# Output pieces inside the recurrent steps, Toeplitz blocks loaded in the mixing stage, first spectrum evacuated by VectorE

## What is computed

```
# layer 0: Fourier mixing and a multilayer perceptron
xf = rfft2(layernorm(x));  o1 = relu(xf @ w1 (per frequency, 8 blocks of 12) + b1)
xs = irfft2(o1);           x = xs + x + gelu(layernorm(xs) @ mlp_w1 + mlp_b1) @ mlp_w2 + mlp_b2
# layer 1: gated Toeplitz convolution along rows and along columns
u, v = silu(srms(x) @ Wu + bu), silu(srms(x) @ Wv + bv)
x = (u * (toeplitz_h(v) + toeplitz_w(v))) @ Wo + bo + x    # coefficients from a small network of positions
# layers 2 and 3: two bidirectional GRUs over the 256 places, forwards and backwards
inner, z = split(layernorm(x) @ w_in.T)
y = silu(bigru_f(inner) + flip(bigru_b(flip(inner)))) * silu(z)
x = x + y @ w_out.T
```

## Time and profile before

| | us |
|---|---|
| median of three runs (1133.48 to 1138.72) | 1134.02 |
| the profiled execution, its own time | 1135.26 |
| its span, first to last instruction | 1133.1 |
| mixing, perceptron, Toeplitz, input of the second layer from last | up to 222 |
| steps of the two recurrent layers | 222 to 645 and 687 to 1109.5 |
| busy: PE 1026.5, DVE 857.8, ACT 783.1, POOL 78.6 | |

### The profile page before, as it was taken

How to read it: one execution, slowest core, us unless ns; L and a number is a source line. 1 busy time by engine, 2 the same in 40 slices (tenths; PEclk the granted TensorE clock), 3 DMA queues, 4 the chain that set the end, 5 groups by cost and what they waited for, 6 DMA issues and landing times. The chain is left out here.

```text
span 1133.1 us, 55089 instructions
## 1 busy us (share of the span) xinstructions
PE 1026.5 (91%) x22248; PEld 850.9 (75%) x22248; DVE 857.8 (76%) x5635; ACT 783.1 (69%) x4511; POOL 78.6 (7%) x149
## 2 busy tenths in 40 slices
PE   3685897899999999999999899999999999999997
PEld 2462687588888888888888667888888888888876
DVE  3645346688888888888888766888888888888883
ACT  4323472687778877777777737878877777777772
POOL 1003130000000000001100000000000001100000
PEclk9577897755555555555555566555555555555555
DMA  4002320000000000000000000000000000000001
GB/s 129 2 2 28 80 62 1 6 4 4 4 3 4 3 4 4 4 4 4 4 3 4 3 6 3 4 4 4 4 3 4 3 4 4 3 4 4 4 4 29
DMA packets 14940, 13.01 MB, mean 11 GB/s; under 512 B 12370, under 2 KB 13843, under 8 KB 14396
## 3 DMA queue, kind: packets, MB, share of 16 engines
q1 hardware_dynamic: 14684, 9.49, 3.7%
HBM read 8.65 MB, written 0.83 MB: 8 GB/s over the span
## 5 line engine op out<-in xcount | busy, mean ns | idle before, releaser
L1103 DVE TENSOR_TENSOR_SCAN L3s_h_hi<-L3s_renew,L3s_terms 96x32 f16<-96x32 f32 x512 | 114.5, 224 | 64.5
L1103 DVE TENSOR_TENSOR_SCAN L2s_h_hi<-L2s_renew,L2s_terms 96x32 f16<-96x32 f32 x512 | 114.4, 224 | 64.6
L1211 PE MATMUL L2s_reset_sum<-L2s_h_hi,L_w_hidden 97*128 97x8 f16 x2048 | 139.8, 179 | 11.7 <-DVEq L1080 0.4
L1211 PE MATMUL L3s_reset_sum<-L3s_h_hi,L_w_hidden 97*128 97x8 f16 x2048 | 139.7, 179 | 11.7 <-DVEq L1080 0.4
L1211 PEld LDWEIGHTS L2s_reset_sum<-L2s_h_hi,L_w_hidden 97*128 97x128 f16 x2048 | 94.6, 107 | 62.3 <-DVE L2s_h_hi L1103 13.7
L1211 PEld LDWEIGHTS L3s_reset_sum<-L3s_h_hi,L_w_hidden 97*128 97x128 f16 x2048 | 94.5, 107 | 62.3 <-DVE L3s_h_hi L1103 13.9
L1159 ACT ACTIVATE L3s_terms<-L3s_cand 96x16 f32<-96x16 f32 x512 | 111.6, 218 | 37.9 <-DVE L3s_cand L1089 6.0
L1159 ACT ACTIVATE L2s_terms<-L2s_cand 96x16 f32<-96x16 f32 x512 | 111.6, 218 | 37.7 <-DVE L2s_cand L1089 5.9
L1211 PE MATMUL L3s_cand_sum<-L3s_h_hi,L_w_hidden 97*128 97x8 f16 x2048 | 131.3, 175 | 4.5 <-DVE L3s_h_hi L1103 3.2
L1211 PE MATMUL L2s_cand_sum<-L2s_h_hi,L_w_hidden 97*128 97x8 f16 x2048 | 131.3, 175 | 4.3 <-DVE L2s_h_hi L1103 2.9
L1211 PE MATMUL L3s_keep_sum<-L3s_h_hi,L_w_hidden 97*128 97x8 f16 x2048 | 130.0, 174 | 0.0
(11 more groups left out here) (262 smaller groups left out, 3233.5 us busy)
## 6 DMA issues: line engine op xcount, KB each, us to landing
L_wih_raw<-in_L_wih SPq DMA_DIRECT2D x2, 1152.0 KB, 11.9
lagged<-in_L_w SPq DMA_DIRECT2D x1, 1296.0 KB
L_w_hidden_raw<-in_L_whh SPq DMA_DIRECT2D x2, 576.0 KB
stream<-in_x SPq DMA_DIRECT2D x2, 384.0 KB, 4.0
out<-stream SPq DMA_DIRECT2D x4, 192.0 KB, 2.1
l_idft<-in_idft SPq DMA_DIRECT2D x1, 400.0 KB
rpe_lw<-in_rpe_lw SPq DMA_DIRECT2D x1, 384.0 KB
lagged<-coefs SPq DMA_DIRECT2D x16, 24.0 KB, 2.0
```

The lines of the kernel that those rows point to most:

```text
L1103: e.tensor_tensor_scan(flat(h_hi[g][0:C, x]), flat(renew[g][:, x]), flat(terms[g][:, x]), 0.0, ALU.mult, ALU.add).then_inc(hi_ready[g], 1)
L1211: return e.matmul(dst, weights.hidden[0:rows, wp, GATES * (2 * g + j) + gate, :], rhs, start=False, stop=False, skip_group_check=True)
```

## The change

- The Toeplitz blocks are stored and loaded in the mixing block: SP waits for `rpe.finished`, stores, waits for ScalarE's clearing of `lagged` (an activation with scale 0, behind its spreads, in place of GpSimd's memset), and issues the 16 transfers. GpSimd's bias addition stays in `mlp`, now first on its list.
- ScalarE waits for the raw weights alone (`raw_loaded`); VectorE evacuates the 8 banks into `spectrum`.
- Toeplitz: results are copied into `values` without transposing (the turning back reads them with a stride of 16 floats instead), and the turning back of a = 0 goes ahead of the products of a = 1; ScalarE's saving goes with it.
- Recurrent steps: GpSimd has nothing left. For chunks from step 128 on, VectorE does 12 pieces of 96x64 in the next chunk, one between `kept_part` and `new_state` of 12 of the 16 half-steps: 4 additions of directions, 4 products y times gate, 4 products with the sigmoid; ScalarE does 4 sigmoids, each behind a tanh. Only the last chunk's pieces stand behind the last step. The output block keeps the projection and the residual sum; the spare products go. `s_tok` lies in `lagged`.

```diff
 # mix_frequencies, SP, VectorE and ScalarE
-                e.dma_start(w_raw, d["L0_w1"]).then_inc(w_loaded, 16)
+                e.dma_start(w_raw, d["L0_w1"]).then_inc(raw_loaded, 16)
...
                 e.dma_start(idft[:], d["idft"]).then_inc(w_loaded, 16)
+                e.wait_ge(rpe.finished, 1)
+                e.dma_start(coefs.rearrange("(m c) a l -> c m a l", m=CHUNKS), coef[:]).then_inc(lagged_loaded, 16)
+                e.wait_ge(lagged_loaded, 16)
+                e.wait_ge(spread_ready_s, CLEARED)
+                for octet in range(8):
+                    mine = slice(octet * SIDE, (octet + 1) * SIDE)
+                    for axis in range(2):
+                        e.dma_start(lagged[mine, axis, :, mine], lagged_layout(coefs, octet, axis)).then_inc(lagged_loaded, 16)
...
+                for b in range(BATCH):
+                    e.wait_ge(transformed, b + 1)
+                    e.tensor_scalar(spectrum[:, :, b], banks[b][0:C, 0:2 * FREQS], affine[:, 0:1], None, ALU.mult).then_inc(evacuated, 1)
...
-                e.wait_ge(w_loaded, 48)
+                e.wait_ge(raw_loaded, 16)
...
-                for b in range(BATCH):
-                    e.wait_ge(transformed, b + 1)
-                    e.activation(spectrum[:, :, b], banks[b][0:C, 0:2 * FREQS], ACT.Copy, scale=affine[:, 0:1])\
-                        .then_inc(evacuated, 1)
...
+                e.activation(lagged[:].rearrange("p a n q -> p (a n q)"), ident[:, 0:1].to_broadcast([P, 2 * OCTETS * P]),
+                             ACT.Copy, scale=0.0).then_inc(spread_ready_s, 1)
 # mlp, GpSimd (SP's store and its 16 loads go from here too)
-                e.memset(lagged[:], 0.0).then_inc(cleared, 1)
 # toeplitz
-        TURNED, VALUES, INNER, BLOCKS_AT, CONV_AT, BACK, OUT = 0, 4, 20, (28, 40), (34, 46), 52, 68
+        TURNED, VALUES, INNER, BLOCKS_AT, CONV_AT, BACK, OUT = 0, 4, 20, (28, 40), (34, 54), (46, 60), 68
...
-                        e.tensor_copy(convolved[axis][:, :, 32 * i:32 * i + 32].rearrange("p w c -> p c w"),
-                                      bank(CONV_AT[a] + i)[:].rearrange("p (c w) -> p c w", w=SIDE)).then_inc(conv_saved, 1)
+                        e.tensor_copy(values[axis][:, i * BANK:(i + 1) * BANK], bank(CONV_AT[a] + i)[:]).then_inc(conv_saved, 1)
...
+                def back(a):
+
+                    e.wait_ge(conv_saved, GROUPS_OF_4 * (a + 1))
+                    for n in range(CHUNKS * NB):
+                        m, k = divmod(n, NB) if a == 0 else (n % CHUNKS, n // CHUNKS)
+                        if a == 0 and n >= 2:
+                            e.wait_ge(block_saved, GROUPS_OF_4 + n - 1)
+                        if a == 1 and n < 2:
+                            e.wait_ge(first_saved, 6 + n + 1)
+                        for j in range(4):
+                            last = e.transpose(bank(BACK[a] + n)[0:C, j * P:(j + 1) * P],
+                                               by_place[ORDER[a]][:, 4 * k + j, m * C:(m + 1) * C], ident[:])
+                        last.then_inc(back_done, 1)
...
 # gru_steps, VectorE
+                def beside(g, q):
+
+                    n, before = 2 * (q % STEPS) + g, q - q % STEPS - STEPS
+                    if before >= SEQ // 2 and n < 12:
+                        (add_directions, apply_y, apply_gate)[n // 4](before, n % 4)
...
                     kept_part(0, q)
+                    beside(0, q)
                     new_state(0, q)
...
+                for work in (add_directions, apply_y, apply_gate):
+                    for i in range(4):
+                        work(SEQ - STEPS, i)
+                e.wait_ge(gated, count(SEQ - STEPS, 3))
...
 # gru_steps, ScalarE
+                        if q >= SEQ // 2 + STEPS and 4 <= 2 * s + g < 8:
+                            sigmoid_of_y(q - s - STEPS, 2 * s + g - 4)
```

142 lines of the change are left out of this document (61 added, 81 removed).

## The result

| | before | after |
|---|---|---|
| median, us | 1134.12 | 1105.47 |
| executions, us | 1133.48 to 1138.72 (4) | 1105.72, 1105.75, 1098.21, 1105.21 |
| profiled execution, us (its span) | 1135.26 (1133.1) | 1105.72 (1103.8) |

The ratio is 0.9728, 95% interval 0.9696 to 0.9760: 2.7% faster. The forecast was 1097, its range 1090 to 1107. The time is inside the range and 8.5 above the forecast. One execution of four was at 1098.21; it has no trace, only a mean granted clock of 0.569 where the three others have 0.562 to 0.564.

The account below looks back on a forecast made before the run. Bound mainly by recurrent half-steps in which TensorE, ScalarE and VectorE hand over small pieces, with chained stages around them. Terms 7.4 + 3.0 + 7.1 + 10.8 + 8.8 = 37.1 off 1134.0 gave about 1097, range 1090 to 1107.

Parts of the forecast that it names:

- its idle time shrinks from 4.76 to 1.0: Toeplitz stage: TensorE's wait before the output product shrinks, the clock stays high; 7.1 gained in all, 2.1 if fallen.
- clock fallen before L824: Toeplitz output product: TensorE's clock is already low when it starts; 5.0 less gained, 1102, chance 0.13.
- Start 7.4: Kernel start: with VectorE evacuating the spectrum, the shift starts at 20.9 instead of 28.31; 7.4 gained.
- The bound of 4.7 for late weights: Kernel start: if raw weights came as late as the inverse DFT, ScalarE ends at 23.8; gain only 4.7.
- Perceptron 3.0: Perceptron's norm: no memset frees 6.46, but GpSimd's bias addition can stop the rows for 3.43; 3.0 gained, bounds 3.0 and 6.4.
- the 3.0 given as a sign: Perceptron: rows would start 3.0 behind the norm's start and stop once for 3.4.
- Toeplitz 7.1: Toeplitz stage: 2.1 from VectorE's pairs starting earlier, 7.1 in all with the output product at the high clock.
- Steps 10.8: Recurrent steps: without GpSimd's pieces, 15 chunks in each of 2 layers save 0.36 each; VectorE's pieces cost 0; 10.8 gained.
- Output 8.8: Output stage: the projection starts at 647.05 instead of 651.44, 4.4 in each of two layers; 8.8 gained.
- The slower rivals: Recurrent steps: additions overrun (1103, chance 0.10); pieces don't overlap `h_hi` (1142, 0.07); the 0.36 isn't GpSimd's (1108, 0.05).
- VectorE keeping the ports: Perceptron: GpSimd's addition gets in only behind VectorE's rows; 3.4 more gained, 1093.5, chance 0.15.
- clock 5.0 and start 2.7 together: Range's upper side: two shortfalls together, the output product's clock (5.0) and the start (2.7), give 1105.

Follow-up runs that it names:

- the kernel with three spare products: Changed kernel, GpSimd's bias addition behind the rows, spare TensorE products: three ahead of L827, two at perceptron's end, three ahead of Toeplitz and perceptron transposes each; median 1095.68.
- the one with late weights: Changed kernel with ScalarE's weights waiting for the inverse DFT again, while VectorE still evacuates the spectrum; 1102.14 and 1106.53.

## Why the prediction came out as it did

The mechanism was right nearly everywhere. The main miss is one step: **"its idle time shrinks from 4.76 to 1.0", so the clock stays at 1.00 through L827, 5.0 gained.** Two readings in it failed. The idle time was 2.47: the transposes ended at 175.86, because strided weights cost nothing (0.114 and not 0.165), while VectorE still needed 5.42 for its first four pairs. The faster the transposes, the longer TensorE waited for the same pairs. And the earlier trace rows was read as a pause that the clock stands: there it fell 184.7 - 182.0 = 2.7 after TensorE had stopped. The prediction took this one fall as a bound for all shorter pauses, and it isn't one. Eleven other traces have a pause of 1.47 or more at this place, and there the clock fell 1.2 (the kernel with three spare products) to 4.1 (the one with late weights) after TensorE had stopped, often when the product was already running. It fell in all of them: wherever the pause was 2.47, the output product took 12.5 to 14.0. With the pause filled the term is 3.9 to 4.9.

Nor would the idle time of 1.0 have been enough for the whole term. The prediction let the second half of L827 start after a wait of 1.5 (189.9 - 184.7 - 3.7) and still run in 3.7. The kernel with three spare products had just this picture, and with it 7.14 for the second half; from the transposes to the next stage it gained 21.85 - 20.29 = 1.6 on the changed kernel, not 5.0.

The rival named for this (clock fallen before L824, chance 0.13, 1102) is what the trace shows, but for the moment: the clock fell as the product began. It was under-weighted. And it was drawn too narrowly. The forecast counted the clock in one stretch and took it in all others as it was in the trace of before, although the change moved every one of them by 7 to 10. Two stretches that had been at the high clock began at the low one and lost 3.3 and 2.1 by it. These 5.3 (10.09 - 4.75) are in no term and no rival.

Point by point:
- *Start 7.4:* the shift gained 7.36, the start of the next block 6.89. The raw weights' landing was read 1.9 too early and was still in time. The bound of 4.7 for late weights was too low a gain: 6.1 by the experiment.
- *Perceptron 3.0:* 3.20, by the mechanism foreseen, a single stop of the rows by GpSimd. The Trainium skill (SBUF — State Buffer, "SBUF: two separate sides") lets the one that starts first keep the shared ports for a whole instruction. The trace agrees: the addition came in between two rows and held them for 3.42. The rows started 2.57 behind the norm's start; the 3.0 given as a sign doesn't agree with the prediction's own 95.0, which makes 2.6. What comes with the stop on TensorE's side, transposes in two parts and a low clock behind them, was overlooked.
- *Toeplitz 7.1:* 3.69. The order gave 3.7 where 2.1 stood; the step that was mis-sized is the transposes' 0.165, taken from L765, whose weights are strided too. Why L765 is slower in its strided half no run shows. The 5.0 was absent.
- *Steps 10.8:* 5.66 in the first layer, and with the additions undone 11.7 came back. Pieces cost nothing; the margin of 0.05 to 0.10 measured 0.07. The piece with the strided write is the 0.27 one, and it is followed after 0.13.
- *Output 8.8:* 4.11 in the first layer; in the second, steps and output and input together 10.52 against 9.8.
- *The sum:* 37.1 - 5.0 (L827) - 5.3 (two stretches) + 1.6 (Toeplitz order) + 0.9 (the rest) = 29.3, which is the trace's difference of spans.

The slower rivals were not near, and neither was VectorE keeping the ports. The range held because "clock 5.0 and start 2.7 together" had been let in. Only half of that happened; the start came nearly in full (6.89 of 7.4), and what took its place is the clock of two other stretches. That the time lies inside the range is in this part luck.

What stays open: why one of eight executions of the changed kernel is at 1098.2. Its mean granted clock is the highest of them, and 7.3 is about what L827 (5.0) and the values' products (2.1) lose together, but it has no trace. It also isn't settled what decides the clock in the perceptron when nothing splits the transposes (8.74 once, 5.42 in the four other traces).

## What to carry to other kernels

A forecast that moves a TensorE stage by some microseconds has to price its clock afresh in each later stretch, as a term with both ends (low and high clock throughout), even where no instruction there is changed. Before an engine's pause is shortened "to nothing", ask which other operation ends that pause: here VectorE's pairs did, and faster transposes only made it longer. And a GpSimd instruction of some length that may fall among VectorE rows should be made to wait for them. Else its own duration is the price, here 3.3, and TensorE's clock may come on top.

## What the runs showed of the hardware

- After a pause of 2.47 ahead of the output product TensorE's clock fell from 1.00 to 0.50 in all nine traces that have it, between the product's first instruction and 1.6 behind it (2.5 to 4.1 after TensorE had stopped), and after one of 1.47 inside L838 the second half ran at 0.50. The pauses of 0.78 and 0.79 ahead of the back transposes L788 left it at 1.00. In the kernel before it fell 2.7 after TensorE had stopped. The Trainium skill (TensorE: Matmul & The Clock Gate, "Part 1: The HAM clock gate") has the chip judge activity at moments that don't restart with the kernel, so that the same kernel varies from one execution to the next; the two traces of the changed kernel agree (values' products 14.61 and 13.57, L827 13.97 and 12.97).
- A delay of 0.96 on VectorE made the kernel 3.7 faster, because the perceptron's products then ran at the high clock (5.42 instead of 8.76) and the values' products too (12.53 instead of 13.57).
- TensorE's transposes with a stationary operand at a stride of 16 floats go at 0.114 to 0.115, as contiguous ones do; VectorE's contiguous copy of the same data takes 0.69 instead of 1.12.
- Nine f16 products of 512 columns and then 13.81 of 96-column products without a pause did not raise the clock from 0.50 behind the steps. The stage behind the Toeplitz stage begins with two f32 products of 512 columns (four instructions, 3.70) and goes on with transposes; there the clock rose 3.6 to 7.4 after the first of them in all fourteen traces.
- GpSimd's 64-element additions, four in 1.28, made the recurrent half-step beside them 1.11 long instead of 0.81.
